# Block attention: weight halves prepared by GpSimd in the first stage; causal mask by a matmul, maxima and exponentials read from PSUM

## The chip, the cores and the metric

One core of a Trainium2 chip runs the whole program. The metric is the device time of one execution in microseconds (us), the median of the runs shown. Engines: PE (TensorE, matmuls), DVE (VectorE), ACT (ScalarE), POOL (GpSimd), SP (SyncE, which here issues every DMA, all on one queue, and computes nothing). In the profile's rows "bank" is one of eight PSUM banks of 128 x 512 fp32.

## The reference, cut to what matters

Two layers over 16 batches of 128 tokens with 256 features. Layer 0: a cross attention with 16 heads of size 8 over features as tokens (its scores are computed per batch element), then a mixture of 64 experts. Layer 1: an mLSTM, then a "block": layer norms, causal self attention with 16 heads of size 128 and rotary embedding, and a mixture of 4 experts. The change touches layer 1's block attention and, as a place for work, layer 0's attention. The block attention is

```python
q = (h @ wq + bq).reshape(b, s, H, HD).transpose(0, 2, 1, 3)      # H, HD = 16, 128; h: (16, 128, 256)
k = (h @ wk + bk).reshape(b, s, H, HD).transpose(0, 2, 1, 3)
v = (h @ wv + bv).reshape(b, s, H, HD).transpose(0, 2, 1, 3)
q = q * cos + _rotate_half(q) * sin
k = k * cos + _rotate_half(k) * sin
scores = jnp.einsum('bhqd,bhkd->bhqk', q, k) / math.sqrt(HD)
scores = jnp.where(causal[None, None], scores, jnp.finfo(jnp.float32).min)
probs = jax.nn.softmax(scores.astype(jnp.float32), axis=-1).astype(q.dtype)
out = jnp.einsum('bhqk,bhkd->bhqd', probs, v)
return out.transpose(0, 2, 1, 3).reshape(b, s, H * HD) @ wo + bo
```

## The kernel before, in words

Each engine has its own instruction list, written out by hand in a fixed order, and waits on semaphores (`wait_ge`). The stages follow each other: layer 0 attention (to about 350 us of the span), layer 0 experts (to about 945), mLSTM (to about 1091), block attention (to about 1689), block experts.

**Two halves.** The large products use fp32r matmuls with both operands split in two: hi, the value rounded to fp32r, and lo, the rest. `product` (line 63) makes three matmuls of it: hi x hi, hi x lo, lo x hi (lines 67, 68, 69). So a weight needs its hi and its lo half in SBUF before it is used.

**First stage, layer 0 attention** (`layer0_*`, lines 112 to 478). For each of the 16 batches PE computes scores twice. The first pass (`maxima`, line 204) gives each row's maximum on DVE; it runs 28 heads (`AHEAD`) ahead of the second pass (`exponentials`, line 232), whose scores ACT exponentiates. The maxima of a batch are turned by PE, copied by ACT, cut into three bf16 parts by POOL (lines 474 to 478, `max_split`), and put by three small DMAs (`max_rows`, line 153, source `a_mparts`) into rows 72 to 74 of the stacked queries `a_qs`, where the second pass adds them inside its matmul: PE waits for `max_in` before a batch's first exponentials. The stacked queries and keys of a batch come from scratch in HBM by six DMAs of 192 KB, three for queries (line 146) and three for keys (line 147), each into 24 partitions (`stack`); four batches are held (`A_RING`). SP's order in the main loop is: three maxima DMAs for batch b, then, once PE has done all exponentials of batch b-1 (`exp_scores`, line 144), the six DMAs of the stack for batch b+3, then the maxima of batch b+1, and so on. POOL does nothing else here once the stacks are prepared.

**Block attention** (`attention_*`, from line 1442). 64 steps, one for each chunk of four batches and each of the 16 heads. In step n PE does, in this order: queries and keys of n (12 matmuls of 512 columns), scores of n-1 (4 fp32 matmuls, two records each; line 1700), the values of one batch (6 of 512), the turning of the probabilities of n-3 (4), the weighing of the values for n-4 (8 records), and the projection of n-5 (12 of 256 columns). Beside them:

- SP loads the raw weights of a head (`b_raw_qk`, 256 KB; `b_raw_o`, 128 KB) three deep, and those of the values of four heads (`b_raw_v`, 512 KB) two deep.
- DVE rounds them to hi (`split_qk`, `split_o`, `split_v`; lines 1872, 1878, 1884), POOL subtracts for lo (`rest`, line 1978).
- ACT writes the half-swapped queries and keys (`b_turned`, line 1809), POOL multiplies them by the sine (line 1996), DVE makes bias plus cosine product (`b_straight`, line 1892) and adds the two (line 1938).
- DVE adds the mask to the scores of n-1 and writes them to SBUF (`b_probs`, line 1907; this frees the score bank), takes the maximum (line 1909) and scales it (line 1911); ACT takes exponentials of n-2 in place (line 1798) with their sums; POOL multiplies by the inverse sums (line 1999).
- DVE and ACT take turns in copying the turned probabilities; ACT rounds the weighed values (line 1837) and DVE makes their rest (line 1948).

Layer norms of later chunks ("input" pieces, from line 1646) and the gate of finished chunks ("gate" pieces) are spread over the steps, one piece a step. Square roots and exponentials need different tables on ACT.

Of the kernel before, what the change touches and what calls it, by code (L numbers as in the profile page):

```python
# [103 lines left out]

def layer0_semaphores(k):
    s = k.sems("a", "weights_in var root normed qk_sums v_sums qk_whole qk_rounded q_rest k_rest q_middle k_middle q_low k_low v_copied k_ones "
               "max_scores maxed max_turned max_copied max_split exp_scores exped cleared weighted sums_copied turned_back divided "
               "out_sums out_turned proj_sums projected added")
    return s, {n: [k.sem(f"a_{n}{i}") for i in range(count)] for n, count in (("q_out", A_SLOTS), ("k_out", A_SLOTS), ("stack_in", A_RING), ("max_in", A_RING))}


def layer0_sp(k, m, s, ring):
# [35 lines left out]

    def max_rows(b):
# [304 lines left out]
def layer0_pool(k, m, s, ring):  # L454
# [16 lines left out]
    for b in range(NB):  # L471
# [6 lines left out]
        pool.tensor_tensor(m.mparts[i][:, 2, :], m.mrow[i][:, :], m.mparts[i][:, 1, :], ALU.subtract).then_inc(s.max_split)  # L478

# [962 lines left out]
def attention_memory(k, stack):  # L1442
    sb = tensors(k, stack, "b")
    pair = lambda name, n: [sb(f"{name}_{half}", [P, n], F32R) for half in ("hi", "lo")]
    m = namedtuple("m", "raw_qk raw_o raw_v split_qk split_o split_v rope mask norm columns v turned straight probs peak peak_scaled total inv probsT outT")
    return m([sb(f"raw_qk{i}", [P, NQK]) for i in range(3)], [sb(f"raw_o{i}", [P, D]) for i in range(3)], [sb(f"raw_v{i}", [P, NV]) for i in range(2)],
             [pair(f"qk{i}", NQK) for i in range(2)], [pair(f"o{i}", D) for i in range(2)], [pair(f"vw{i}", NV) for i in range(2)],
             sb("rope", [P, 2, S]), sb("mask", [P, S]), norm_memory(sb, "first"), sb("first_columns", [P, DK, BANK]),
             [sb(f"v{i}", [P, CHUNK, GROUP * RD]) for i in range(2)], [sb(f"turned{i}", [P, 2, BANK]) for i in range(2)],
             [sb(f"straight{i}", [P, 2, BANK]) for i in range(2)], [sb(f"probs{i}", [P, CHUNK, S]) for i in range(3)],  # L1450
             *([sb(f"{n}{i}", [P, CHUNK]) for i in range(2)] for n in ("peak", "peak_scaled", "total", "inv")),
# [3 lines left out]
def block_semaphores(k):  # L1455
    s = k.sems("b", "small_in tables_in gate_in experts_in pad var root normed rows turned columns x_hi x_lo with_bo qk_hi qk_lo o_hi o_lo v_hi v_lo "
               "qk_sums qk_turned qk_straight qk_sine rotated score_sums masked peaked exps inverted normalised probs_turned probs_by_dve probs_by_act v_sums v_copied weighed "
# [836 lines left out]
```

## Time and profile before

| | us |
|---|---|
| median of 3 runs | 1828.59 |
| lowest, highest | 1820.28, 1829.84 |
| the profiled execution | 1817.43 |
| its span | 1816.1 |

The profile describes one execution, which is shorter than each of the runs in the table. Busy times of the engines lie beside each other. In its chain of waits each step goes back to what released the instruction; in rows of the timeline the square bracket is the idle time of the engine before the instruction and what ended it; "x" is how many instructions a row merges.

### The profile page before, as it was taken

Reading aid. Unit: us, or ns where it says so; the run is one execution under the profiler, and the core shown is the slowest. Engines: PE = TensorE matmul, PEld = TensorE weight load, DVE = VectorE, ACT = ScalarE, POOL = GpSimd, SP = SyncE. Lnnn points to the kernel's source line nnn. Section 1 sums busy time; section 2 is a strip of 40 time slices with the busy share of each in tenths; the row PEclk is TensorE's granted clock in tenths of the full one; section 3 lists DMA queues with packets and bytes.
Section 4 is the critical chain, followed back from the end, with each engine's and each line's share of the span. In section 5 each row is a group of like instructions: output and inputs, shape, how many; then the busy total and the mean of one; then the engine's idle time right before and its main releaser. Section 6 shows DMA issues by size and latency. Waiting matters only on the chain.

```text
span 1816.1 us, 30483 instructions
## 1 busy us (share of the span) xinstructions
PE 1606.5 (88%) x10932; PEld 1268.4 (70%) x10932; DVE 1259.6 (69%) x2321; ACT 1019.4 (56%) x2050; POOL 765.8 (42%) x575
## 2 busy tenths in 40 slices
PE   4379999789999999999986964899899999999898
PEld 2135555368888888888872533788787778888687
DVE  6458788378644455444445576999999999999454
ACT  4247777644433335333335653877776877677453
POOL 5200000024435333333330014798798688877000
PEclk9569899899999999999996987999999999999899
DMA  5613232243343333343400002123112111211220
GB/s 155 154 55 83 76 84 61 80 111 105 94 129 106 104 110 102 108 116 102 118 10 6 4 2 92 48 72 103 56 56 68 56 56 56 68 48 30 70 47 24
DMA packets 73349, 137.42 MB, mean 76 GB/s; under 512 B 12824, under 2 KB 41308, under 8 KB 70384
## 3 DMA queue, kind: packets, MB, share of 16 engines
q1 hardware_dynamic: 73200, 135.48, 26.4%
q8 instruction: 88, 1.44, 0.3%
q14 instruction: 61, 0.50, 0.1%
HBM read 125.70 MB, written 8.95 MB: 74 GB/s over the span
## 4 chain that ended last, share of the span: by engine, by line
PE 54%; DVE 19%; issue 9%; DMA 8%; ACT 6%; POOL 2%; SPq 1%; DVEq 0%; ACTq 0%; POOLq 0%
PE bank L67 13%; PE bank L69 13%; PE bank L68 13%; DMA a_qs<-a_mparts 5%; DVE b_straight L1938 3%; DVE b_straight L1892 2%; PE bank L246 2%; PE bank L232 2%; PE bank L204 2%; ACT b_turned L1809 2%; DVE b_peak L1909 2%; POOL e_hidden L944 1%; DVE b_probs L1907 1%; PE bank L1700 1%; PE bank L1732 1%
## 5 line engine op out<-in xcount | busy, mean ns | idle before, releaser
L944 POOL TENSOR_TENSOR e_hidden<-e_gated,e_comb_wide 128x512 f32<-128x512 f32 x132 | 211.0, 1599 | 346.7 <-DVE e_gated L909 331.1
L784 ACT CAST e_hidden_hi<-e_hidden 128x512 fp32r<-128x512 f32 x132 | 82.0, 622 | 320.6 <-POOL e_hidden L944 320.6
L902 DVE TENSOR_TENSOR e_hidden_lo<-e_hidden,e_hidden_hi 128x512 fp32r<-128x512 f32 x132 | 98.2, 744 | 209.8 <-ACT e_hidden_hi L784 209.8
L423 DVE TENSOR_REDUCE a_negmax<-bank 128x2 f32<-128x512 f32 x256 | 165.6, 684 | 64.6 <-PE bank L204 63.3
L69 PE MATMUL bank<-e_x_hi,e_weights_lo 128*128 128x512 f32 (+1 forms) x528 | 209.5, 397 | 0.0
L67 PE MATMUL bank<-e_x_hi,e_weights_hi 128*128 128x512 f32 (+1 forms) x528 | 208.4, 395 | 0.7 <-ACT e_comb_rows L744 0.7
L68 PE MATMUL bank<-e_x_lo,e_weights_hi 128*128 128x512 f32 (+1 forms) x528 | 208.4, 395 | 0.0
L1809 ACT ACTIVATE b_turned<-bank,b_swap_bias 64x512 f32<-64x512 f32 x256 | 174.9, 683 | 17.7 <-PE bank L69 12.9
L1996 POOL TENSOR_TENSOR b_turned<-b_turned,b_rope 128x512 f32<-128x512 f32 x128 | 167.5, 1329 | 5.3 <-ACT b_turned L1809 4.8
L340 ACT ACTIVATE a_exp<-bank 128x512 f32<-128x512 f32 x256 | 142.9, 596 | 42.8 <-PE bank L232 35.4
L69 PE MATMUL bank<-e_weights_hi,e_hidden_lo 128*128 128x256 f32 (+1 forms) x528 | 149.4, 283 | 0.0
L67 PE MATMUL bank<-e_weights_hi,e_hidden_hi 128*128 128x256 f32 (+1 forms) x528 | 148.2, 281 | 0.5 <-DVE e_hidden_lo L902 0.5
L68 PE MATMUL bank<-e_weights_lo,e_hidden_hi 128*128 128x256 f32 (+1 forms) x528 | 148.4, 281 | 0.0
L1938 DVE TENSOR_TENSOR b_straight<-b_straight,b_turned 128x512 f32<-128x512 f32 x128 | 140.5, 1136 | 0.0
L1798 ACT ACTIVATE b_probs<-b_probs,b_peak_scaled 128x128 f32<-128x128 f32 x256 | 99.7, 391 | 68.2 <-DVE b_peak_scaled L1911 68.1
L204 PE MATMUL bank<-a_ks,a_qs 72*128 72x256 bf16 x512 | 108.0, 297 | 31.0 <-DMA a_ks<-a_k_parts 13.2
L1978 POOL TENSOR_TENSOR b_qk_lo<-b_raw_qk,b_qk_hi 128x512 fp32r<-128x512 f32 x64 | 84.7, 1324 | 109.9 <-DVE b_qk_hi L1872 109.9
L909 DVE TENSOR_TENSOR e_gated<-e_silu,bank 128x512 f32<-128x512 f32 x132 | 90.5, 686 | 56.7 <-PE bank L69 44.2
L232 PE MATMUL bank<-a_qs,a_ks 75*128 75x256 bf16 x512 | 100.2, 280 | 21.0 <-DMA a_qs<-a_mparts 20.1
L69 PEld LDWEIGHTS bank<-e_x_hi,e_weights_lo 128*128 128x128 f32 (+1 forms) x528 | 98.7, 187 | 22.7
L67 PE MATMUL bank<-b_x_hi,b_qk_hi 128*128 128x512 f32 x256 | 103.0, 402 | 12.8 <-POOL b_qk_lo L1978 4.5
L67 PEld LDWEIGHTS bank<-e_x_hi,e_weights_hi 128*128 128x128 f32 (+1 forms) x528 | 99.4, 188 | 19.7 <-ACT e_comb_rows L744 1.1
(326 smaller groups left out, 4318.1 us busy)
## 6 DMA issues: line engine op xcount, KB each, us to landing
e_comb_wide<-e_combT SPq DMA_DIRECT2D x130, 256.0 KB, 4.0
e_raw<-in_e_weights SPq DMA_DIRECT2D x64, 384.0 KB, 4.5
b_raw_qk<-in_b_wqk SPq DMA_DIRECT2D x64, 256.0 KB, 2.8
a_qs<-a_q_parts SPq DMA_DIRECT2D x48, 192.0 KB
a_ks<-a_k_parts SPq DMA_DIRECT2D x48, 192.0 KB
b_raw_v<-in_b_wv SPq DMA_DIRECT2D x16, 512.0 KB, 3.8
b_raw_o<-in_b_wo SPq DMA_DIRECT2D x64, 128.0 KB, 2.0
moe_comb_wide<-b_comb_rows SPq DMA_DIRECT2D x16, 256.0 KB, 6.7
```

Of the source, the lines that this page charges most:

```text
L67: pe.matmul(out, w_hi, x_hi, start=start, stop=False, skip_group_check=True)
L68: pe.matmul(out, w_hi, x_lo, start=False, stop=False, skip_group_check=True)
L69: return pe.matmul(out, w_lo, x_hi, start=False, stop=stop, skip_group_check=True)
L204: last = pe.matmul(bank[:, qb * POS:(qb + 1) * POS], m.qs[r][0:TERM_ROWS, h, qb * P:(qb + 1) * P], m.ks[r][0:TERM_ROWS, h, :], start=True, ...
L232: last = pe.matmul(bank[:, kb * POS:(kb + 1) * POS], m.ks[r][0:ROWS, h, kb * P:(kb + 1) * P], m.qs[r][0:ROWS, h, :], start=True, stop=True)
L340: act.activation(m.expo[at % A_EXPS][:, :, :].rearrange("p k q -> p (k q)"), banks[2 + h % 2][:, :], ACT.Exp, scale=float(1 / np.sqrt(np.f ...
L423: dve.tensor_reduce(m.negmax[b % 2][:, h, :], banks[h % 2][:, :].rearrange("p (q n) -> p q n", q=2), AX.X, ALU.max, negate=True).then_inc( ...
L944: pool.tensor_tensor(m.hidden[i][0:rows, :], m.gated[i][0:rows, :], m.comb_wide[u % E_RING][0:rows, chunk * BANK:(chunk + 1) * BANK], ALU. ...
L1798: last = act.activation(w.probs[n % 3][:, b, :], w.probs[n % 3][:, b, :], ACT.Exp, scale=SCALE, bias=w.peak_scaled[i][:, b:b + 1], accum_o ...
L1809: last = act.activation(w.turned[i][dst:dst + half, which, :], banks[bank][src:src + half, :], ACT.Identity, bias=m.swap_bias[dst:dst + ha ...
L1938: dve.tensor_tensor(w.straight[n % 2][:, which, :], w.straight[n % 2][:, which, :], w.turned[n % 2][:, which, :], ALU.add).then_inc(s.rotated)
L1996: pool.tensor_tensor(x, x, w.rope[:, 1, :].unsqueeze(1).to_broadcast([P, CHUNK, S]), ALU.mult).then_inc(s.qk_sine)
```

## The change

**In the first stage**, 32 pieces of the block attention's weights (16 heads' qk, 8 half groups of v, 8 pairs of o; 256 KB each) are loaded into four slots of the otherwise unused `columns` tensor, split by POOL into a rounded copy and a rest, and both are stored to scratch in HBM (256 KB each). POOL does two pieces behind each batch's `max_split`; SP does the stores of the batch before and the loads of the batch after in `max_rows`.

```diff
+KEPT, KEPT_SLOTS, KEPT_EACH = 512, 4, 2
+def kept_of(b):
+    return range(KEPT_EACH * b, min(KEPT_EACH * (b + 1), 2 * RH))
 def layer0_sp(k, m, s, ring):
+    def load_kept(u):
+        r = u % KEPT_SLOTS
+        if u >= KEPT_SLOTS:
+            sp.wait_ge(ring["kept_out"][r], 2 * DMA * (u // KEPT_SLOTS))
+        sp.dma_start(kept_places(k, u, units[u][0].shape)[0], units[u][0]).then_inc(ring["kept_in"][r], DMA)
+    def store_kept(u):
+        low, high = kept_places(k, u, units[u][0].shape)
+        sp.wait_ge(s.kept_low, u + 1)
+        for dst, src in zip(units[u][1], (high, low)):
+            sp.dma_start(dst, src).then_inc(ring["kept_out"][u % KEPT_SLOTS], DMA)
+    def kept(b):
+        if b:
+            for u in kept_of(b - 1):
+                store_kept(u)
+            for u in kept_of(b + 1):
+                load_kept(u)
     def max_rows(b):
...
+        kept(b)
...
     for b in range(1, A_RING):
         stack(b)
+    for u in range(KEPT_SLOTS):
+        load_kept(u)
...
+    for u in kept_of(NB - 1):
+        store_kept(u)
+    for r in range(KEPT_SLOTS):
+        sp.wait_ge(ring["kept_out"][r], 2 * DMA * (2 * RH // KEPT_SLOTS))
 def layer0_pool(k, m, s, ring):
         pool.tensor_tensor(m.mparts[i][:, 2, :], m.mrow[i][:, :], m.mparts[i][:, 1, :], ALU.subtract).then_inc(s.max_split)
+        for u in kept_of(b):
+            whole, high = kept_places(k, u, (P, KEPT))
+            pool.wait_ge(ring["kept_in"][u % KEPT_SLOTS], DMA * (u // KEPT_SLOTS + 1))
+            pool.tensor_copy(high.bitcast(F32R), whole).then_inc(s.kept_high)
+            pool.wait_ge(s.kept_high, u + 1)
+            pool.tensor_tensor(whole.bitcast(F32R), whole, high, ALU.subtract).then_inc(s.kept_low)
```

**In the block attention**, SP fetches both halves straight into their two buffers, and the splitting on DVE and POOL goes. A fetch waits until PE has done with the buffer. The mask, as bf16, is added by a matmul of the identity that opens the score bank; the scale 1/sqrt(128) goes into the queries' rotary tables (`rope_q`); DVE's maximum and ACT's exponentials read the bank, which PE may overwrite only once the exponentials are done. ACT's wait for the small vectors moves from the stage's start to the input's piece 6.

```diff
 def attention_sp(k, m, w, s, ring, before):
+    def fetch(split, whole, n, fetched):
+        for i in range(2):
+            sp.dma_start(split[n % 2][i][:, :].bitcast(F32), whole[n % whole.shape[0], i]).then_inc(fetched[n % 2], DMA)
...
-        if n + 3 < B_STEPS:
-            load_qk(n + 3)
-        if 4 <= n <= B_STEPS:
-            load_o(n - 1)
-        if n % GROUP == 0 and n // GROUP + 2 < B_GROUPS:
-            load_v(n // GROUP + 2)
+        if 2 <= n + 1 < B_STEPS and n >= 1:
+            sp.wait_ge(s.qk_sums, 2 * n)
+            fetch(w.split_qk, k.qk_parts, n + 1, ring["qk_in"])
+        if 2 <= n - 4 < B_STEPS:
+            sp.wait_ge(s.proj_sums, n - 5)
+            fetch(w.split_o, k.o_parts, n - 4, ring["o_in"])
+        if n % GROUP == 0 and 2 <= n // GROUP + 1 < B_GROUPS:
+            sp.wait_ge(s.v_sums, n)
+            fetch(w.split_v, k.v_parts, n // GROUP + 1, ring["v_in"])
     def scores(n):
+        if n:
+            pe.wait_ge(s.exps, n)
+        else:
+            pe.wait_ge(s.constants, 2)
+        pe.matmul(banks[SC][:, :].rearrange("p (b s) -> p b s", b=CHUNK), w.ident_16[:, :], w.mask_16[:, :].unsqueeze(1).to_broadcast([P, CHUNK, S]),
+                  start=True, stop=False, skip_group_check=True)
         pe.wait_ge(s.rotated, 2 * (n + 1))
-        if n:
-            pe.wait_ge(s.masked, n)
...
     def exponentials(n):
...
-            last = act.activation(w.probs[n % 3][:, b, :], w.probs[n % 3][:, b, :], ACT.Exp, scale=SCALE, bias=w.peak_scaled[i][:, b:b + 1],
+            last = act.activation(w.probs[n % 3][:, b, :], banks[SC][:, b * S:(b + 1) * S], ACT.Exp, bias=w.peak[i][:, b:b + 1],
...
-    act.wait_ge(s.small_in, 4 * DMA)
     for piece in range(INPUT_PIECES):
+        if piece == 6:
+            act.wait_ge(s.small_in, 4 * DMA)
         input_chunk(0, piece)
...
-        dve.tensor_tensor(probs[:, :, :], by_batch(banks[SC][:, :]), w.mask[:, :].unsqueeze(1).to_broadcast([P, CHUNK, S]), ALU.add).then_inc(s.masked)
-        dve.wait_ge(s.masked, n + 1)
-        dve.tensor_reduce(w.peak[i][:, :], probs[:, :, :], AX.X, ALU.max, negate=True).then_inc(own.tick())
-        dve.wait_ge(own.sem, own.n)
-        dve.tensor_scalar(w.peak_scaled[i][:, :], w.peak[i][:, :], SCALE, None, ALU.mult).then_inc(s.peaked)
+    def peaks(n):
+        dve.wait_ge(s.score_sums, n + 1)
+        dve.tensor_reduce(w.peak[n % 2][:, :], by_batch(banks[SC][:, :]), AX.X, ALU.max, negate=True).then_inc(s.peaked)
```

## Rows read from the trace of the kernel before

**Rows 1.** The page: busy us, share of the span; the chain's shares by line.
```profile
PE 1606.5 (88%) x10932; PEld 1268.4 (70%) x10932; DVE 1259.6 (69%) x2321; ACT 1019.4 (56%) x2050; POOL 765.8 (42%) x575
PE bank L67 13%; PE bank L69 13%; PE bank L68 13%; DMA a_qs<-a_mparts 5%; DVE b_straight L1938 3%; DVE b_straight L1892 2%; PE bank L246 2%; PE bank L232 2%; PE bank L204 2%; ACT b_turned L1809 2%; DVE b_peak L1909 2%; POOL e_hidden L944 1%; DVE b_probs L1907 1%; PE bank L1700 1%; PE bank L1732 1%
```
**Rows 2.** Busy us in one stretch: PE, PEld, DVE, ACT, POOL, PE clock, DMA share, GB/s.
```profile
1270.00:1400.00 130.00, 118.98 (x741) 103.19 (x740) 127.27 (x227) 95.02 (x228) 107.79 (x79) 0.99 0.19 56
```
**Rows 3.** Timeline of SP's queue, first stage: start us, duration us, engine, line.
```profile
139.57 0.76 SPq L146 DMA_DIRECT2D a_qs<-a_q_parts  x1
146.82 1.83 SPq L153 DMA_DIRECT2D a_qs<-a_mparts  x3
154.34 0.75 SPq L146 DMA_DIRECT2D a_qs<-a_q_parts  x1
218.39 0.75 SPq L146 DMA_DIRECT2D a_qs<-a_q_parts  x1
```
**Rows 4.** Chain that ended last, first stage: start us, duration us, what.
```profile
148.06 8.04 DMA a_qs<-a_mparts
```
**Rows 5.** Timeline of PE, first exponentials of four batches.
```profile
140.91 0.39 PE L232 MATMUL bank<-a_qs,a_ks 75*128 75x256 bf16 x2 [0.97 <-DMA a_qs<-a_mparts]
156.15 0.39 PE L232 MATMUL bank<-a_qs,a_ks 75*128 75x256 bf16 x2 [1.43 <-DMA a_qs<-a_mparts]
200.70 0.61 PE L232 MATMUL bank<-a_qs,a_ks 75*128 75x256 bf16 x2 [2.13 <-DMA a_qs<-a_mparts]
306.05 0.39 PE L232 MATMUL bank<-a_qs,a_ks 75*128 75x256 bf16 x2 [0.89 <-DMA a_qs<-a_mparts]
```
**Rows 6.** Line 153 from 117 to 120 us, no stack in flight.
```profile
DMA to landing us min/median/max: 1.8/1.9/1.9
```
**Rows 7.** Busy us in stretches of the first stage, columns as in rows 2.
```profile
142.00:144.00 2.00, 2.00 (x27) 1.17 (x18) 1.17 (x3) 1.49 (x4) 0.00 (x0) 1.00 0.60 147
150.00:152.00 2.00, 2.00 (x19) 1.67 (x16) 1.74 (x5) 1.99 (x5) 0.00 (x0) 1.00 0.19 70
201.00:211.00 10.00, 10.00 (x65) 5.10 (x64) 4.29 (x8) 4.92 (x11) 1.11 (x3) 0.53 0.32 94
```
**Rows 8.** Timeline of PE, score matmuls of four block steps.
```profile
1121.91 1.16 PE L1700 MATMUL bank<-b_straight 128*128 128x128 f32 x8 [1.97 <-DVE b_straight L1938]
1239.40 1.05 PE L1700 MATMUL bank<-b_straight 128*128 128x128 f32 x8
1247.24 1.06 PE L1700 MATMUL bank<-b_straight 128*128 128x128 f32 x8
1672.80 1.16 PE L1700 MATMUL bank<-b_straight 128*128 128x128 f32 x8 [1.05 <-DVE b_straight L1938]
```
**Rows 9.** Groups by form, 1060 to 1620 us, DVE: busy us, mean ns | idle before.
```profile
L1872 DVE CAST b_qk_hi<-b_raw_qk 128x512 fp32r<-128x512 f32 x59 | 44.4, 753 | 0.0
L1911 DVE TENSOR_SCALAR b_peak_scaled<-b_peak 128x4 f32<-128x4 f32 x56 | 40.7, 726 | 1.9
L1907 DVE TENSOR_TENSOR b_probs<-bank,b_mask 128x512 f32<-128x512 f32 x56 | 36.8, 657 | 0.0
```
**Rows 10.** The page's groups, POOL.
```profile
L1978 POOL TENSOR_TENSOR b_qk_lo<-b_raw_qk,b_qk_hi 128x512 fp32r<-128x512 f32 x64 | 84.7, 1324 | 109.9 <-DVE b_qk_hi L1872 109.9
```
**Rows 11.** Chain that ended last, mLSTM stage, a bf16 matmul of 128x512.
```profile
1006.91 0.32 PE bank L1225
```
**Rows 12.** Timeline of ACT, one table load.
```profile
1284.58 1.28 ACT L1778 ACT_TABLE_LOAD   x1
```
**Rows 13.** Timeline of DVE at the start of the block attention.
```profile
1097.46 0.18 DVE L1657 RECIPROCAL b_first_rstd<-b_first_rstd 128x4 f32<-128x4 f32 x1 [4.06 <-ACT b_first_rstd L1778]
1117.87 3.99 DVE L1938 TENSOR_TENSOR b_straight<-b_straight,b_turned 128x512 f32<-128x512 f32 x2
```
**Rows 14.** The DMA view: the queue (packets, MB, share of 16 engines); an issue (us to landing).
```profile
q1 hardware_dynamic: 73200, 135.48, 26.4%
out<-resid SPq DMA_DIRECT2D x8, 256.0 KB, 2.2
```

More of the change, by code:

```diff
@@ L102, in layer0_memory, with kept_units, kept_places @@
         [sb(f"rstd{i}", [P, CHUNK]) for i in range(NCHUNK)])
+KEPT, KEPT_SLOTS, KEPT_EACH = 512, 4, 2
+def kept_units(k):
+    io, units = k.io, []
+    for h in range(RH):
+        units.append((io["b_wqk"][h], [k.qk_parts[h, i] for i in range(2)]))
+    for g in range(RH // GROUP):
+        for half in range(2):
+            cols = slice(half * KEPT, (half + 1) * KEPT)
+            units.append((io["b_wv"][g][:, cols], [k.v_parts[g, i][:, cols] for i in range(2)]))
+    for h in range(0, RH, 2):
+        units.append((io["b_wo"][h:h + 2].rearrange("h p n -> p h n"), [k.o_parts[h:h + 2, i].rearrange("h p n -> p h n") for i in range(2)]))
+    return units
+def kept_places(k, u, shape):
+    first = (u % KEPT_SLOTS) * 2 * KEPT
+    whole, high = (k.columns[:, :, :].rearrange("p k t -> p (k t)")[:, at:at + KEPT] for at in (first, first + KEPT))
+    return [t if len(shape) == 2 else t.rearrange("p (h n) -> p h n", h=shape[1]) for t in (whole, high)]
+def kept_of(b):
+    return range(KEPT_EACH * b, min(KEPT_EACH * (b + 1), 2 * RH))
 def layer0_semaphores(k):
@@ L1444, in attention_memory @@
     pair = lambda name, n: [sb(f"{name}_{half}", [P, n], F32R) for half in ("hi", "lo")]
[L1445 to L1448, printed above, removed]
+    m = namedtuple("m", "split_qk split_o split_v rope rope_q mask mask_16 ident_16 norm columns v turned straight probs peak total inv probsT outT")
@@ L1449, in attention_memory @@
+    return m([pair(f"qk{i}", NQK) for i in range(2)], [pair(f"o{i}", D) for i in range(2)], [pair(f"vw{i}", NV) for i in range(2)],
+             sb("rope", [P, 2, S]), sb("rope_q", [P, 2, S]), sb("mask", [P, S]), sb("mask_16", [P, S], BF16), sb("ident_16", [P, P], BF16), norm_memory(sb, "first"), sb("first_columns", [P, DK, BANK]),
              [sb(f"v{i}", [P, CHUNK, GROUP * RD]) for i in range(2)], [sb(f"turned{i}", [P, 2, BANK]) for i in range(2)],
              [sb(f"straight{i}", [P, 2, BANK]) for i in range(2)], [sb(f"probs{i}", [P, CHUNK, S]) for i in range(3)],
-             *([sb(f"{n}{i}", [P, CHUNK]) for i in range(2)] for n in ("peak", "peak_scaled", "total", "inv")),
+             *([sb(f"{n}{i}", [P, CHUNK]) for i in range(2)] for n in ("peak", "total", "inv")),
@@ L1683, in queries_keys @@
         pe.wait_ge(s.x_lo, chunk + 1)
-        pe.wait_ge(s.qk_lo, n + 1)
+        pe.wait_ge(ring["qk_in"][n % 2], 2 * DMA * (n // 2 + 1))
         for which, bank in ((0, Q), (1, K)):
@@ L1707, in values @@
         b = chunk * CHUNK + tile
-        pe.wait_ge(s.v_lo, group + 1)
+        pe.wait_ge(ring["v_in"][group % 2], 2 * DMA * (group // 2 + 1))
         if free:
@@ L1739, in project @@
         pe.wait_ge(s.out_lo, n + 1)
-        pe.wait_ge(s.o_lo, n + 1)
+        pe.wait_ge(ring["o_in"][n % 2], 2 * DMA * (n // 2 + 1))
         if h == 0 and chunk:
@@ L1987, in attention_pool @@
         input_chunk(0, piece)
-    pool.wait_ge(s.tables_in, 2 * DMA)
+    pool.wait_ge(s.constants, 2)
     for n in range(B_STEPS + 5):
-        if n + 1 < B_STEPS:
-            rest(w.raw_qk, w.split_qk, s.qk_hi, s.qk_lo, n + 1)
         if n < B_STEPS:
@@ L1995, in attention_pool @@
                 x = by_batch(w.turned[n % 2][:, which, :])
[L1996 removed]
+                pool.tensor_tensor(x, x, (w.rope if which else w.rope_q)[:, 1, :].unsqueeze(1).to_broadcast([P, CHUNK, S]), ALU.mult).then_inc(s.qk_sine)
         if 2 <= n <= B_STEPS + 1:
```

93 lines of the change are left out of this document (25 added, 68 removed).

## The prediction

> **What bounds the kernel now.** I read the page's busy shares first [rows 1]: PE is busy 88% of the span and no other engine is near it, but that mean covers five stages, and the change touches two. The page's chain of waits names one item that is no engine: 5% of the span, some 90 us, is the DMA that brings the maxima rows [rows 1]. Then the busy time by stretches [rows 2]: in the block stage DVE is busy 127.27 of 130 us (98%) where PE is busy 118.98, so DVE sets that pace.
>
> *The first stage's loop* is seen by laying three views side by side. SP issues the six DMAs of a stack at 139.57 and the three small maxima DMAs at 146.82 [rows 3]; the third of these lands only 8.04 us after its issue, at 156.10, and PE's next exponentials start at 156.15, after 1.43 us of idle [rows 4, 5]. The same small DMAs with no stack ahead of them land in 1.8 to 1.9 us [rows 6]. What holds them is the stack: the DMA share is 0.60 at 142 to 144 and 0.19 at 150 to 152 [rows 7], there some three of sixteen engines at work. So a stack's bytes lie unevenly, a few engines carry most of them, and the maxima wait behind these. PE is idle before the exponentials for that DMA in ten steady batches by 0.29 to 2.13 us [rows 5], so this loop has no slack: stack issued, about 15.8 us later the maxima land (139.57 to 156.15 is 16.6; ten such pairs run from 15.0 to 16.6, mean 15.8) [rows 3, 5], the batch of exponentials runs, the next stack goes out at 154.34, and so on. From the landing at 140.91 to that at 306.05 are 11 batches: 165.1 / 11 = 15.0 us each [rows 5].
>
> *The block stage.* PE's first score matmul comes 64 times, from 1121.91 to 1672.80: 550.9 / 63 = 8.74 us a step; its shortest steps are 7.84 us (1239.40 to 1247.24), and they recur whenever DVE is not late [rows 8]. So 7.84 us is PE's own work.
>
> **The change, block stage.** DVE loses per step the rounding of qk (753 ns), the mask addition (657) and the scaling of the peak (726) [rows 9], 2.1 us, and the rounding of o and a quarter of v beside: 98% of 8.74 is 8.6 us of DVE work, and at most 6.4 of it is left. The maximum now reads PSUM instead of SBUF; the addition that goes away read the same bank in 657 ns, so I cost it at 0, within 0.1 either way, and not on PE's path. POOL loses as many subtractions (1324 ns for qk) and keeps three operations of that size, 4.0 us [rows 10]. ACT keeps its instructions: 95.02 of 130 us [rows 2], 6.4 a step. The exponentials' source moves from SBUF to PSUM, cost 0: ACT has 1.7 us of room in 8.1, and 0.1 us either way on each of four fits in it. PE gains one 128x512 bf16 matmul per step. Such a matmul holds the chain for 0.32 us in the mLSTM stage [rows 11], the upper end; nearest below is one record of the eight score matmuls, 1.06 / 8 = 0.13 [rows 8]. I take 0.25, nearer to the one of its own shape. PE becomes the bound at 7.84 + 0.25 = 8.1 us.
>
> New waits there: the mask matmul waits until ACT has read the scores of the step before. ACT starts these after its out_hi, which follows the weighing; until the mask matmul PE still has the projection and the queries/keys, 24 of its 50 matmuls and so about 4 us, while ACT has five of its dozen instructions, about 2.5. That cover is gone only where a pair of table loads (2 x 1.28) [rows 12] stands between; nine such places at 1 us: up to 9, I take 5. The loads of both halves are issued once the step before last has left its buffer, 13 us ahead, for about 4 us of transfer. They double the stage's traffic from a share of 0.19 [rows 2] to about 0.4, which costs nothing.
>
> Sum: 63 steps x 8.1 = 510; the first four lack the weighing and the projection, a quarter of PE's work, about -6; side pieces on PE, some 30 small matmuls a chunk at 0.13 (1.06 / 8), three chunks, 12; table loads 5. That is 521 against 551: -30. At the stage's start ACT waits for the b_bo DMA, and DVE, its variance done, stands idle 4.06 us for ACT's root of 0.2 [rows 13]; the wait moves to a later piece: -3.8. The first two additions take 3.99 us beside POOL's subtractions [rows 13]; half of it should go: -2. The drain's five mask additions and scalings mostly ride beside PE: 0. Three small constants on DVE lie beside PE's first products. Together -36, between -44 (no table trouble, 7.96 us steps) and -20.
>
> **The change, first stage.** Added are 32 pieces: 32 loads and 64 stores of 256 KB on SP's one queue, and 64 POOL operations of 128x512. POOL first: its rows give 1.3 us for such an operation [rows 10], 5.3 a batch, in an engine that works 1.1 us a batch. It stands behind the maxima's split and is done long before the next one. Cost 0.
>
> SP's queue is the point. After the maxima DMAs of batch b it now (1) issues the four stores of batch b-1, (2) waits until each pair has landed, since the two loads for batch b+1 go into the same slots, (3) issues these, and only then (4) the next stack. The stores spread over all 16 engines, so a share of each lies behind the old stack and the maxima on the few slow ones: none is complete before the maxima landing M. A 256 KB store alone lands in 2.2 us against 1.9 for the 8 KB maxima: at least 0.3 us each; the page's 135.48 MB in 26.4% of 1816.1 us are 283 GB/s: 0.9 each [rows 6, 14]. I take 0.7, nearer to the page's mean over all transfers. Four stores: M + 2.8; the last load's issue 0.45, so the stack goes out at M + 3.3, where now it goes out 1.3 to 1.8 us before M. Then 15.8 us as now, and 0.3 for the load just ahead: the next M is 19.4 later, not 15.0. PE's batch (under 15, and 17.7 in the batch with the lowered clock: 200.70 to 218.39) [rows 3, 5] fits inside. So +4.4 us for each of 11 batches: +48. The first four loads stand between the first stacks and the first maxima: 4 x 0.7 = 2.8. Sum +51; with 0.3 a DMA (2.4 x 11 + 1.2) +28, with 0.9 (5.2 x 11 + 3.6) +61. Behind the last stack (three batches) nothing is held, and the closing wait for the stores ends before the experts' loads may start.
>
> The Trainium skill, "DMA: Bandwidth & Descriptors", section "Queues, rings and completion order", says that each DMA engine takes its descriptors in ring order and that a DMA's semaphore is complete only with all its engines; section "How many engines (k)" there, that a transfer is split over the largest number up to 16 that divides the slowest dimension of both sides, which for 3x8 rows would be 3 engines, for 128 rows 16. The 0.17 to 0.27 of rows 7 agrees; by that rule the stores are all held as I say, and without it (stores passing the stack) the first rival's sum holds.
>
> **Total.** 1817.4 us (span 1816.1) + 51 - 36 = 1832. The profiled execution was 11 us under the median of the runs shown, so 1844 beside 1828.6.
>
> **Rivals.**
> 1. *The stores are not held, and the block's gain stands alone.* SP now has 5.7 us between the third maxima DMA (148.65) and the next stack (154.34) [rows 3]. If the four stores land within about 3.5 us of the last issue, the stack is in time. That is the point of decision: a stack issue no later than PE's end of the batch. For it: a lone store lands in 2.2 [rows 14]. Against it: 6.9 to 8.7 us for maxima on the same queue at the same place. 1828.6 - 36 + 3 = 1796.
> 2. *The clock falls with the new idle.* After 2.13 us of idle at 200.70 the granted clock was 0.53 in 201 to 211 and that batch took 17.7 us instead of 13.4 [rows 3, 5, 7]. With over 4 us of idle in each batch it may stay low through one; twice 13.4 less what DVE and ACT hide is about 23, so 11 x (23 - 19.4) = 40 more: 1884.
> 3. *The block's PE does not reach its floor*: ACT in order, exponentials at its head, a late qk_turned in each step. 1828.6 + 51 = 1880, if nothing is gained. Against it: ACT was busy 95 of 130 us [rows 2].
> 4. *The weights' halves arrive late in the block* (two buffers, not three): about 1 us a step, 1828.6 + 51 - 36 + 60 = 1904; 13 us of lead speaks against it.
>
> **How the numbers follow.** Forecast 0.62, its own range 1813 to 1862 (the two sets of bounds); rival 1 0.20; rival 2 0.08; rival 3 0.08; rival 4 0.02. What a measurement of this kernel can tell is about 0.5%, 9 us: 1819 to 1838 is "same". The forecast's share is 0.03 faster, 0.10 same, 0.49 slower. So faster 0.23, same 0.10, slower 0.67. The range 1808 to 1881 takes in rival 3 and leaves out rival 1's centre and most of rival 2.
>
> **What will show it.** In SP's timeline the stack issue some 3 us after the maxima landing, and 19 to 20 us between batches' exponentials, PE idle 4 us or more before each; score matmuls in the block 8.0 to 8.2 us apart, DVE under 80% there; the block's first matmul about 4 us sooner after its start. Wrong: batches still at 15 us (rival 1), a clock of 0.5 through whole batches (rival 2), block steps above 8.5 (rivals 3 and 4).

## The result and the profile after

| | before | after |
|---|---|---|
| median of 18 runs each, us | 1822.62 (1805.01 to 1833.87) | 1830.82 (1826.04 to 1841.5) |
| ratio after / before, 95% interval | | 1.0062 [1.0039, 1.0086] |
| profiled execution: span, us | 1816.1 | 1828.1 |
| experts' first load issued (end of the first stage) | 350.45 | 391.76 (+41.3) |
| block's first load issued | 1091.38 | 1134.52 (+43.1) |
| first / last score matmul of the block | 1121.91 / 1672.80 | 1158.11 / 1682.27 (+36.2 / +9.5) |

The change made the kernel slower by 0.6%: 8 us between the medians, 12 between the profiled executions. The 12 are the sum of a loss of 41.3 us in the first stage, 1.8 in the stages between, 2.5 in the tail behind the block's last scores, and of gains of 6.9 us at the block's start and of 26.7 us over its 63 steps.

The page after: busy times, the clock in 40 slices, the queue and the chain, which answer to [rows 1, 14].
```profile
PE 1633.9 (89%) x10996; PEld 1279.5 (70%) x10996; DVE 1103.7 (60%) x2052; ACT 1007.5 (55%) x2050; POOL 609.9 (33%) x495
PEclk9568888889999999999998787899999999999799
q1 hardware_dynamic: 110832, 194.21, 35.9%
PE 69%; DMA 8%; DVE 7%; ACT 5%; issue 5%; SPq 3%; POOL 3%; POOLq 0%; ACTq 0%; DVEq 0%
```
The same two lines, the clock and the chain, before:
```profile
PEclk9569899899999999999996987999999999999899
PE 54%; DVE 19%; issue 9%; DMA 8%; ACT 6%; POOL 2%; SPq 1%; DVEq 0%; ACTq 0%; POOLq 0%
```
DVE and POOL lost 156 us of work each, and yet the end came later. DVE fell from 19% to 7% of the chain and PE took its place. The DMA had its 8% before, too; SP's queue rose from 1% to 3%.

The timeline of SP's queue in the first stage after, which answers to [rows 3] (start us, duration us, engine, line). L175 is the query stack, L184 the loads of the pieces, L190 their stores, L204 the maxima.
```profile
135.45 2.72 SPq L204 DMA_DIRECT2D a_qs<-a_mparts  x3
138.21 2.09 SPq L190 DMA_DIRECT2D b_qk_parts<-columns  x4
145.33 1.56 SPq L184 DMA_DIRECT2D columns<-in_b_wqk  x2
147.00 0.77 SPq L175 DMA_DIRECT2D a_qs<-a_q_parts  x1
151.93 2.85 SPq L204 DMA_DIRECT2D a_qs<-a_mparts  x3
154.82 2.23 SPq L190 DMA_DIRECT2D b_qk_parts<-columns  x4
164.17 2.29 SPq L184 DMA_DIRECT2D columns<-in_b_wqk  x2
166.57 0.77 SPq L175 DMA_DIRECT2D a_qs<-a_q_parts  x1
```
PE's first exponentials of four batches after, which answer to [rows 5]:
```profile
144.56 0.39 PE L290 MATMUL bank<-a_qs,a_ks 75*128 75x256 bf16 x2 [1.22 <-DMA a_qs<-a_mparts]
163.44 0.61 PE L290 MATMUL bank<-a_qs,a_ks 75*128 75x256 bf16 x2 [3.70 <-DMA a_qs<-a_mparts]
182.56 0.39 PE L290 MATMUL bank<-a_qs,a_ks 75*128 75x256 bf16 x2 [1.20 <-DMA a_qs<-a_mparts]
...
343.78 0.61 PE L290 MATMUL bank<-a_qs,a_ks 75*128 75x256 bf16 x2 [2.51 <-DMA a_qs<-a_mparts]
```
The maxima land at 144.56. The loads go out 0.8 us later, when the stores of 138.21 have landed, and the stack at 147.00; before, it went out 1.3 us ahead of the landing. From 144.56 to 343.78 are 11 batches of 18.1 us, where they were 15.0. Ahead of all of them but one PE waits for the maxima, by 0.22 to 4.38 us, so the loop of the queue still sets the pace.

The block after, by stretches (PE, PEld, DVE, ACT, POOL, clock, DMA share, GB/s; answers to [rows 2]), and, in PE's timeline, two of its steps (answers to [rows 8]).
```profile
1200.00:1300.00 100.00, 99.11 (x631) 85.95 (x630) 66.20 (x100) 74.47 (x188) 48.10 (x38) 1.00 0.46 148
```
```profile
1237.07 1.05 PE L1758 MATMUL bank<-b_straight 128*128 128x128 f32 x8
1245.16 1.05 PE L1758 MATMUL bank<-b_straight 128*128 128x128 f32 x8
```
DVE fell from 98% to 66%; PE, at 99%, is the bound, with 8.09 us from step to step (before, the shortest steps were 7.84 and the mean was 8.74).

### The profile page after: what moved, and what is told of

It reads as the page before. It is cut to its first block, busy times and chain, and to the rows that moved or that the text cites. A ratio compares the mean times of both kernels' runs of the same rounds, so it can differ in the third digit from the quotient of the medians.

```text
span 1828.1 us, 30253 instructions
## 1 busy us (share of the span) xinstructions
PE 1633.9 (89%) x10996; PEld 1279.5 (70%) x10996; DVE 1103.7 (60%) x2052; ACT 1007.5 (55%) x2050; POOL 609.9 (33%) x495
## 4 chain that ended last, share of the span: by engine, by line
PE 69%; DMA 8%; DVE 7%; ACT 5%; issue 5%; SPq 3%; POOL 3%; POOLq 0%; ACTq 0%; DVEq 0%
PE bank L67 16%; PE bank L69 16%; PE bank L68 16%; DMA a_qs<-a_mparts 6%; PE bank L1790 3%; PE bank L1758 3%; PE bank L304 2%; PE bank L290 2%; PE bank L262 2%; PE bank L1780 1%; POOL e_hidden L1008 1%; PE bank L1290 1%; PE bank L1289 1%; SPq L204 1%; PE bank L1300 1%
## 5 line engine op out<-in xcount | busy, mean ns | idle before, releaser
L1869 ACT ACTIVATE b_turned<-bank,b_swap_bias 64x512 f32<-64x512 f32 x256 | 174.9, 683 | 43.1 <-PE bank L69 39.3
L2018 POOL TENSOR_TENSOR b_turned<-b_turned,b_rope_q 128x512 f32<-128x512 f32 x64 | 82.8, 1294 | 258.8 <-ACT b_turned L1869 258.8
L290 PE MATMUL bank<-a_qs,a_ks 75*128 75x256 bf16 x512 | 108.0, 298 | 41.1 <-DMA a_qs<-a_mparts 40.2
L262 PE MATMUL bank<-a_ks,a_qs 72*128 72x256 bf16 x512 | 114.5, 312 | 33.0 <-DMA a_ks<-a_k_parts 13.7
L1935 DVE SCALAR_TENSOR_TENSOR b_straight<-bank,b_head_bias,b_rope_q 128x512 f32<-128x512 f32 x64 | 48.0, 749 | 111.2 <-ACT b_turned L1869 111.1
L68 PEld LDWEIGHTS bank<-e_x_lo,e_weights_hi 128*128 128x128 f32 (+1 forms) x528 | 98.7, 187 | 18.8
```

Source lines behind the costliest of these rows:

```text
L68: pe.matmul(out, w_hi, x_lo, start=False, stop=False, skip_group_check=True)
L262: last = pe.matmul(bank[:, qb * POS:(qb + 1) * POS], m.qs[r][0:TERM_ROWS, h, qb * P:(qb + 1) * P], m.ks[r][0:TERM_ROWS, h, :], start=True, ...
L290: last = pe.matmul(bank[:, kb * POS:(kb + 1) * POS], m.ks[r][0:ROWS, h, kb * P:(kb + 1) * P], m.qs[r][0:ROWS, h, :], start=True, stop=True)
L1869: last = act.activation(w.turned[i][dst:dst + half, which, :], banks[bank][src:src + half, :], ACT.Identity, bias=m.swap_bias[dst:dst + ha ...
```

## The experiments

**Each half of the change alone.** *first_stage_alone* is the kernel before with the 32 pieces (loads, POOL's operations, stores), which nothing reads; *block_alone* is the changed block with the first stage of before. Its scratch is filled in the experts stage by 64 stores of a finished tile, so the halves hold other values than the weights':
```diff
+                if u < 32:
+                    for i in range(2):
+                        sp.dma_start(fills(k, i)[u], m.x_split[1][:, 0, 0:512].bitcast(F32)).then_inc(ring["fill"][(2 * u + i) % 4], DMA)
```


> The kernel before with only the first stage's part of the change (32 pieces loaded, split by GpSimd and stored; nothing reads them later). Theory (SP waits for stores that are held behind the stack on a few DMA engines, so each next stack goes out late): batches 18.1 us apart instead of 15.0, the experts' first load 41 us later than in the kernel before, all later stages unchanged, total +41 us. Rival (the first stage is only part of it; the doubled traffic or the clock of later stages costs too): this kernel is less than 30 us slower than before.

> The changed block attention with the first stage as before; its halves' scratch is filled by 64 stores of a finished tile during the experts stage, so the values are not the weights' halves. Theory: steps of 8.09 us and the earlier start give 27 + 7 us, total -34 against before, the experts stage within 3 us. Rival (part of the block's 27 us comes from POOL and DMA work having been moved, or from the clock): outside -25 to -40.

Measured: 1860.87 us, ratio to before 1.0239 [1.0192, 1.0285], and 1787.46, ratio 0.9835 [0.9791, 0.9879]. Against the 1820.45 us of before beside them that is +40.4 and -33.0; they sum to +7.4, and the whole change measured +8.2: no action of the halves on each other is seen, to within the 8 to 9 us that each interval leaves. In the profiles the first stage alone has batches of 18.3 us and the experts' first load 41.7 us later than before; the block alone has its 63 steps in 522.8 us (550.9 before). Both are what the first theories said. How much one profiled execution differs from another shows in *block_alone*, too: its first stage is that of the kernel before, and it ended 4.7 us later (355.10 instead of 350.45).

**POOL's part of the first stage alone** (*pool_only*: the 64 operations, none of the DMAs; the slots are filled with ones by one GpSimd instruction at the program's start).

> The kernel before, with GpSimd's 64 additional operations of the first stage alone: the same two operations on the same two places of SBUF for each of the 32 pieces, but none of the loads and stores of the pieces, so the places hold no weights. Theory A (GpSimd has the room, and all of the first stage's loss came from the DMA queue): batches of 15.0 us as before and the kernel within 4 us of the kernel before. Theory B (GpSimd's new work slows VectorE, with which it shares SBUF, or delays its own work for the keys): batches of 15.5 us or more and 8 us or more above the kernel before.

Measured: 1825.18 us, ratio 1.0013 [0.9983, 1.0042]; the batches 15.1 us. The first stage is 2.2 us longer, all of it ahead of the first exponentials (113.20 instead of 110.93), where this kernel alone has that fill, 3.54 us. The loss is the queue's, not GpSimd's.

**Eight rows a DMA** (*before_spread*, *after_spread*: each query DMA of a stack cut in three).
```diff
-            sp.dma_start(flat(m.qs[r], 3 * t, 3), parts_of("q")[t].unsqueeze(0).broadcast_to([3, HD, HEADS * POS])).then_inc(ring["stack_in"][r], DMA)
+            for j in range(3):
+                sp.dma_start(flat(m.qs[r], 3 * t + j, 1), parts_of("q")[t]).then_inc(ring["stack_in"][r], DMA)
```


> The kernel before with each query DMA of a stack (24 rows, source repeated three times) issued as three DMAs of 8 rows; the same bytes. Theory (a few engines carry most of the stack and the maxima DMAs wait behind it): the stack's bytes lie on more engines, the maxima land before PE ends the batch, no idle before the first exponentials, batches 13.4 to 13.8 us apart instead of 15.0, the first exponentials some 5 to 8 us earlier, total -20 to -25 us. Rival (PE bounds this stage and the maxima's wait costs nothing more than the 1 us seen): at most -5 us, or slower by SP's twelve issues instead of six.

> The changed kernel with the stack's query DMAs split in the same way. Theory: the stores are no longer held, SP's wait ends before PE ends the batch, batches 13.6 to 14.5 us apart instead of 18.1, total -45 to -55 against the changed kernel, so about -40 against before. Rival (SP's wait for the stores alone is the cost, whatever lies on the engines): batches stay above 16.5 us, gain under 20 us.

Measured: 1811.55 us, ratio 0.9979 [0.9949, 1.0009], batches of 14.2 us; and 1812.15, ratio to before 0.9961 [0.9928, 0.9994], batches of 17.2, some 18 us under the changed kernel. The first isn't clear of the noise (9 us between the medians, 12 between the profiled spans), and of the second it is the rival's numbers that came (batches above 16.5 us, under 20 us gained). The theory, by which the cut frees the queue, failed in both. The stretches from the stack's issue on show why, for before and before_spread (columns as above):
```profile
143.00:145.00 2.00, 2.00 (x18) 1.37 (x15) 1.88 (x5) 1.69 (x4) 0.00 (x0) 1.00 0.71 135
149.00:151.00 2.00, 2.00 (x24) 1.50 (x15) 1.29 (x3) 1.58 (x5) 0.00 (x0) 1.00 0.25 85
151.00:153.00 2.00, 2.00 (x26) 1.08 (x24) 1.80 (x6) 1.90 (x4) 0.00 (x0) 1.00 0.17 70
```
```profile
138.00:140.00 2.00, 2.00 (x18) 1.47 (x17) 1.70 (x5) 1.69 (x4) 0.00 (x0) 1.00 0.68 82
140.00:142.00 2.00, 2.00 (x27) 1.07 (x25) 1.44 (x3) 1.60 (x6) 1.12 (x3) 1.00 0.86 107
146.00:148.00 2.00, 2.00 (x26) 1.24 (x26) 1.80 (x5) 1.99 (x5) 0.00 (x0) 1.00 0.51 74
```
Before ends in a tail of three busy engines (0.17 of 16), each 8 KB packet in 0.31 us. The eight-row DMAs keep 8 to 14 engines busy and move no more: most of their packets take 0.6 to 1.4 us. (Only in the stack's first 2 us, 136 to 138, did they move 147 GB/s, at a share of 0.83.) From its first to its last 8 KB packet a stack takes 12.9 us before and 12.3 in before_spread, the mean of twelve each. So the idle engines were not all of it, and the cut cost nearly what it brought.

**Another order of the stack's rows** (*before_by_dim*, *after_by_dim*): same six DMAs of 24 rows on the same places, but a source with 8 outermost. `q` with `broadcast_to([3, HD, ...])` reads the eight rows three times over; `broadcast_to([HD, 3, ...])` reads each row three times in a row. The keys change their order with the queries, since the two must match.
```diff
-            sp.dma_start(flat(m.qs[r], 3 * t, 3), parts_of("q")[t].unsqueeze(0).broadcast_to([3, HD, HEADS * POS])).then_inc(ring["stack_in"][r], DMA)
-            sp.dma_start(flat(m.ks[r], 3 * t, 3), parts_of("k")).then_inc(ring["stack_in"][r], DMA)
+            sp.dma_start(flat(m.qs[r], 3 * t, 3), parts_of("q")[t].unsqueeze(1).broadcast_to([HD, 3, HEADS * POS])).then_inc(ring["stack_in"][r], DMA)
+            sp.dma_start(flat(m.ks[r], 3 * t, 3), parts_of("k").rearrange("t d f -> d t f")).then_inc(ring["stack_in"][r], DMA)
```


> The kernel before, with the rows of the stacks in another order: within each group of 24 rows the eight dimensions of a head are the outer index and the three repeats the inner one, for queries and keys alike. Number, size and destination of the DMAs (six of 24 rows of 8 KB) stay, the sum over rows is the same; only the outermost dimension of the source is 8 where it was 3. In the kernel before, a stack's packets go at 17 to 20 a microsecond at first and end in a tail in which three DMA engines alone are busy, 12.9 us in all. Theory A (the query DMAs, whose source has 3 as its outermost dimension, run on three engines, and these set the stack's time): the tail goes, the stack needs about 8 us, the maxima behind it are not late any more, PE's batches are at their work of 13.5 to 14.5 us where they were 15.0, and the kernel gains 8 to 20 us. Theory B (the few SBUF rows that a 24-row DMA reaches set the time, or the query's rows being read three times): the destinations are the same, so nothing changes beyond 3 us.

Measured: 1779.65 us, ratio 0.9773 [0.9735, 0.9811]: 41 us less in the medians and 33 between the profiled spans (1816.1 and 1782.8), where at most 20 was expected. The stack's stretches, and SP's queue:
```profile
123.00:125.00 2.00, 2.00 (x17) 1.47 (x18) 1.62 (x5) 1.64 (x4) 0.00 (x0) 1.00 0.55 193
125.00:127.00 2.00, 2.00 (x26) 1.05 (x25) 1.44 (x4) 1.60 (x6) 1.07 (x3) 1.00 0.52 152
127.00:129.00 2.00, 2.00 (x22) 1.20 (x23) 1.97 (x6) 1.91 (x4) 0.05 (x1) 1.00 0.55 150
129.00:131.00 2.00, 2.00 (x28) 1.38 (x17) 1.29 (x4) 1.58 (x4) 0.00 (x0) 1.00 0.31 82
131.00:133.00 2.00, 2.00 (x24) 1.31 (x26) 1.81 (x6) 1.99 (x5) 0.00 (x0) 1.00 0.03 6
```
```profile
127.08 1.82 SPq L153 DMA_DIRECT2D a_qs<-a_mparts  x3
134.59 0.71 SPq L146 DMA_DIRECT2D a_qs<-a_q_parts  x1
140.86 1.19 SPq L153 DMA_DIRECT2D a_qs<-a_mparts  x2
```
Some eight engines (0.52 to 0.55 of 16) carry it at 150 to 193 GB/s, and the long tail of three is gone: a stack takes 8.4 us from its first to its last 8 KB packet, the mean of twelve, and not 12.9. Maxima go out every 13.8 us (the last row shows two of three), and from 100 us on PE never waits for them, where it waited 20.1 us before, 10.0 of these ahead of the first batch. It is busy 100.00 us of 100 at clock 1.00 between 100 and 200, and every batch from 107 to 286 takes 13.8 us: that is PE's own work, and the queue sets the pace no longer. The first stage is 34 us shorter. The batches give 13.5 of these, within the 8 to 20 expected. 19 lie ahead of the first exponentials (91.88 instead of 110.93), behind the first four stacks; that is what the expectation had left out. The Trainium skill, "DMA: Bandwidth & Descriptors", section "Why a DMA increments its semaphore by 16 and not by 1", under "How many engines (k)", says that a DMA goes over the largest number of engines up to 16 that divides the slowest dimension of both its sides. By that rule it would be, as an estimate, 8 for this source and 3 for the old one of the queries, and the shares of 0.55 and 0.17 agree. As queries and keys changed together, what each gave isn't known.

> The changed kernel with the stacks' rows in the order that gained 40 us on the kernel before (query DMAs with 8 as the outermost dimension of their source, where it was 3). Theory A (in the changed kernel too the stack's landing, 12.9 us, and the maxima behind it are in every batch's circle, and the shorter stack leaves room for the pieces): batches of 13.5 to 15 us where they were 18.1, and 40 to 60 us less than the changed kernel, so 1770 to 1790. Theory B (the pieces' own traffic is what holds the batches): batches of 16 us and more, and less than 30 us gained.

Measured: 1761.46 us, ratio to before 0.969 [0.9644, 0.9736], some 68 us under the changed kernel, where 40 to 60 were expected; batches of 14.35, within theory A's 13.5 to 15. Between the two kernels with the new order the first stage differs by 12.0 us (experts' first load at 316.43 and 328.48) where it differed by 41.3: with the new order the change is a gain (0.969 against 0.9773 without the change, 15 us, and 15 between the profiled spans; the two intervals just touch). Of the 12.0 us, 6.0 lie ahead of the first exponentials, and most of the rest in one batch of 17.91 at a granted clock of 0.72; nearly all others take 13.8 to 14.2. Most of what the pieces cost was the tail. That the gain is 15 and not the block's 34 less 12 comes from the untouched stages between, which took 6 us more in this profiled execution (746.0 and 739.8).

**The loads a batch later** (*late_loads*: the changed kernel; the loads stand ahead of the stores, behind the next maxima).
```diff
+        if b >= 2:
+            for u in kept_of(b):
+                load_kept(u)
         if b:
             for u in kept_of(b - 1):
                 store_kept(u)
-            for u in kept_of(b + 1):
-                load_kept(u)
```


> The changed kernel, with the loads of a batch's two kept pieces issued one batch later, ahead of that batch's stores: SP then never waits for stores that it has only just issued. Amounts and sizes of all DMAs stay. In the changed kernel the stack went out 2.4 to 3.1 us after the maxima had landed and a batch took 18.1 us. Theory A (a batch is the time until the stack goes out, plus the stack's landing, plus the maxima behind it): the stack goes out within 1 us of the release of its ring place, a batch takes 16 to 17 us, and the kernel is 12 to 22 us faster than the changed kernel. Theory B (what the pieces move through the same queue lengthens the stack and the maxima, whenever it is issued): the batches stay within 0.4 us of 18.1, and the kernel within 5 us of the changed one.

Measured: 1808.65 us, ratio to before 0.9928 [0.9889, 0.9967], 22 us under the changed kernel, at theory A's upper end; batches of 16.3 us, PE's wait for the maxima 27.8 us between 100 and 350 instead of 40.2. So 1.8 of the 3.1 us that a batch had grown were SP's wait for its own stores. What the remaining 1.3 are isn't shown. In two of the 11 batches, of 18.6 and 18.9 us, the granted clock was 0.73 (before, in one of 17.9, it was 0.72), and the one behind the first of them took 18.0. The other eight take 15.5 in the mean, where before without its slow one took 14.7, so the pieces' traffic in the queue explains 0.8 us of a batch at most.

**The mask on VectorE again** (*dve_mask*: the changed kernel without the mask matmul; VectorE adds the mask and writes the scores to SBUF, and its maximum and ACT's exponentials read them there).
```diff
-        pe.matmul(banks[SC][:, :].rearrange("p (b s) -> p b s", b=CHUNK), w.ident_16[:, :], w.mask_16[:, :].unsqueeze(1).to_broadcast([P, CHUNK, S]),
-                  start=True, stop=False, skip_group_check=True)
+        dve.tensor_tensor(probs[:, :, :], by_batch(banks[SC][:, :]), w.mask[:, :].unsqueeze(1).to_broadcast([P, CHUNK, S]), ALU.add).then_inc(s.masked)
```


> The changed kernel, with the causal mask added by VectorE into SBUF as in the kernel before, maxima and exponentials read from there, and no mask matmul on TensorE; the weights' halves still come ready-made. In the changed kernel most score steps take 8.09 us, which is PE's own work with the mask matmul of 0.39 us in it, and PE waits 9.1 us in all for the exponentials ahead of that matmul. Theory A (PE is the bound and VectorE at 92 per cent just fits): steps of 7.85 us at most places, and 5 to 15 us less than the changed kernel. Theory B (VectorE, with 0.8 us more of work in each step, is the bound or hands its results to PE late): steps of 8.1 us and more, no gain or up to 15 us more than the changed kernel.

Measured: 1809.86 us, ratio to before 0.9938 [0.9907, 0.997], 21 us under the changed kernel (16 between the profiled spans, 1828.1 and 1812.0), above the 5 to 15 expected. Steps of 7.83 us in PE's timeline:
```profile
1238.20 1.06 PE L1754 MATMUL bank<-b_straight 128*128 128x128 f32 x8
1246.03 1.06 PE L1754 MATMUL bank<-b_straight 128*128 128x128 f32 x8
```
63 steps take 505.8 us instead of 524.2. VectorE, the bound before, has room for the addition (busy 70.80 us of the 100 from 1200 on); put on PE, the bound after, it costs 18 us. In these 18 are two things that no run separates: the matmul's own place in the step, 0.26 us (8.09 less 7.83), and PE's wait ahead of it until the exponentials have been read from the bank, 9.1 us in all. With the mask on VectorE that wait is gone, and 2.6 us of waiting for `b_straight` come in its place.

**The edits together** (*by_dim_late_loads*, and with the mask on VectorE).

> The changed kernel with the stacks' rows in the new order and the pieces' loads one batch later, mask on TensorE as changed. If the two edits of the first stage act on one circle, the second has little left to gain: 0 to 8 us less than with the new order alone, batches of 13.4 to 14 us. If SP's wait for its own stores still holds the stack back by 2 to 3 us a batch, the loads' place gains 15 us or more. Expected 1760 to 1785, 35 to 60 us under the kernel before.

> The kernel of the run before it in this call, with the mask added by VectorE into SBUF and no mask matmul. On the changed kernel this edit gained 15 to 20 us. If that gain belongs to the block alone, it is found again whole here: 1745 to 1770. If it was in part a clock or an overlap that came with the slow first stage, it is less than 8 us.

Measured: 1765.06 us, ratio 0.9714 [0.9665, 0.9763], batches of 13.8: the loads' place brings nothing that can be measured on top of the row order. With the mask on VectorE 1751.09, ratio 0.9627 [0.958, 0.9674], 14 us less, and 63 steps in 504.6 us where they were 522.3: the block's gain of 18 us is found again in the steps, and this kernel is 68 us under the one before and some 79 under the changed one.

**Rows nine apart** (*before_strided*: what slowed the eight-row DMAs? 18 DMAs of eight rows stand in place of the six).
```diff
+            for j in range(3):
+                rows = slice(3 * t + j, TERM_ROWS, 9)
+                sp.dma_start(m.qs[r][rows, :, :].rearrange("p h n -> p (h n)"), parts_of("q")[t]).then_inc(ring["stack_in"][r], DMA)
+                sp.dma_start(m.ks[r][rows, :, :].rearrange("p h n -> p (h n)"), parts_of("k")[j]).then_inc(ring["stack_in"][r], DMA)
```


> The kernel before, its stacks loaded by 18 DMAs of eight rows of 8 KB (nine for the queries as in before_spread, nine for the keys, where that kernel has three of 24 rows), and the eight rows of each lie nine SBUF rows apart instead of side by side. In before_spread the DMA engines were busier than in the kernel before (share 0.68 to 0.86 in the first 4 us) and moved less (82 to 107 GB/s), and the batches were 14.1 us. Theory A (eight neighbouring rows are what makes a packet slow): with rows spread over 72 partitions 150 GB/s and more, the stack in 8 to 9 us, batches of 13.8 us and PE without idle time ahead of the exponentials, 15 us and more under before_spread, so 1780 to 1795. Theory B (the number of DMAs, or reading the same few rows of DRAM from several engines, makes it slow): 80 to 110 GB/s again, batches of 14.1 us and more, within 8 us of before_spread or above it (18 issues on SP take 6 us of each batch).

Measured: 1815.38 us, ratio 0.9983 [0.9951, 1.0015], batches of 14.35. Theory B's numbers came (its 80 to 110 GB/s, batches of 14.1 us and more, within 8 us of before_spread), and of its causes the number of DMAs, by another way than slow packets: the packets are quick again (0.31 to 0.55 us), yet through most of the stack only 78 to 119 GB/s move, with a share of 0.26 to 0.41, because each issue holds SP for 0.60 us, 18 of them 11.6 us and not the 6 that I had counted:
```profile
141.76 0.60 SPq L148 DMA_DIRECT2D a_qs<-a_q_parts  x1
142.40 0.60 SPq L149 DMA_DIRECT2D a_ks<-a_k_parts  x1
```
With some 5 engines at work instead of 8 to 14 the quick packets may come from the rows' distance or from the smaller crowd. What slows eight neighbouring rows stays open. The Trainium skill, "SBUF — State Buffer", "Door 1: The DMA port swizzle (why `[64,N]` ≈ `[32,N]`)", has a formula from the partition to one of 16 ports, by which eight neighbouring rows that start at a multiple of eight lie on two; the runs fit it and don't prove it.

## Why the prediction was right

The forecast was 1844 us beside 1828.6, slower by 0.8%; measured were 1830.82 beside 1822.62, slower by 0.45% (0.6% by the ratio). In the profiled executions the forecast was +15 us (+51 - 36), and +12.0 came. Path and cause were right in both stages. That the sum came so near is in part luck: the first stage was forecast 10 us too dear, the block's gain 2 us too large, and 4 us came that the sum didn't have. The effect is the small difference of two large ones and barely above the 0.5% that the prediction called "same".

- *First loads, +2.8:* +3.4 (first exponentials at 110.93 and 114.33).
- *A batch of 19.4 us, +48 over 11:* 18.1 us, +34.1. This is the term that was too large, by both of its parts: the stack at M + 3.3 was at M + 2.4 to 3.1 in the four batches from 144.56 on, mean 2.6, so a store cost nearer to 0.5 than to 0.7; and the 16.1 from there to the next maxima were 18.1 - 2.6 = 15.5. Its direction and cause stand by *late_loads* (SP's wait) and by the new order: in *after_by_dim* the loads go out 5.0 to 6.6 us after the stores' first issue (five batches from 106.19 on; 134.67 and 141.28 are one such pair), in the changed kernel 7.1 to 9.7 us (five from 138.21 on). Its lower bound is summed wrong: 0.3 a DMA instead of 0.7 takes 1.6 from the 4.4 and leaves 2.8, not 2.4, so +32 and not +28. Nor do the bounds give the forecast's own range: 1828.6 + 61 - 20 is 1870, not 1862. Neither changes the forecast.
- *Behind the last stack nothing is held, 0:* +3.6 (M of batch 13 to the experts' first load 44.4 and 48.0 us), so here the prediction left a term out, and it is the clock. Behind the idle time of 2.51 us at 343.78 PE was busy without a gap to 361.68, 17.9 us at a mean granted clock of 0.72; before, that batch took 13.6 at 1.00 (306.05 to 319.68). With it the first stage is 3.4 + 34.1 + 3.6 = 41.1, of the 51 forecast, within its bounds of 28 to 61.
- *POOL 0:* right by *pool_only*, batches of 15.1 beside 15.0.
- *Three engines carry most of a stack, by the share of 0.17 to 0.27:* right for the tail, and worth more than I saw. (Rows 7 show 0.19 of it; in the stack's second half, from 147 to 153, the share was 0.17 to 0.25, three to four engines.) I used it for the place of the stores only and did not ask what the tail cost the kernel before: 41 us.
- *PE's floor in the block 7.84 + 0.25 = 8.1:* 8.09. The mask matmul's own record is longer, 389 ns: records of neighbouring matmuls overlap (those of 128x512 beside a step last 0.39 us and start every 0.23). The last figures of each row are the idle time before it and what ended it:
```profile
L1754 PE MATMUL bank<-b_mask,b_ident 128*128 128x512 bf16 x62 | 24.1, 389 | 9.3 <-ACT b_probs L1858 9.1
L1858 ACT ACTIVATE b_probs<-bank,b_peak 128x128 f32<-128x128 f32 x248 | 87.4, 371 | 2.2 <-DVE b_peak L1947 2.0
```
- *Table loads in front of the mask matmul, 5 of at most 9:* 9.1 us, the upper end, at eight places (2.31 at one and 0.88 to 1.19 at seven). *Steps 521 us:* 524.2, so -26.7 and not -30.
- *Start of the block -3.8 and -2:* -6.9. The wait for ACT's root fell from 4.06 to 0.33 us, the first two additions from 3.99 to 1.82:
```profile
1136.89 0.18 DVE L1711 RECIPROCAL b_first_rstd<-b_first_rstd 128x4 f32<-128x4 f32 x1 [0.33 <-ACT b_first_rstd L1836]
1155.99 1.82 DVE L1968 TENSOR_TENSOR b_straight<-b_straight,b_turned 128x512 f32<-128x512 f32 x2
```
- *Exponentials from PSUM, 0:* right for the time. An exponential went from 391 to 371 ns and its accumulator read from 188 to 212.
- *Not in the sum:* +1.8 us in the stages between and +2.5 in the tail.

The rivals. *Not held* (1796): the stores were complete only after the maxima had landed (loads issued at 145.33); refuted by SP's timeline. *The clock stays low* (1884): half of it came. The granted clock of 100 to 300 us fell from 0.91 and 0.95 to 0.81 and 0.83, and the batches were still 18.1 us: PE's batch at that clock still fits behind the DMAs, if only just (ahead of one batch PE waited 0.22 us, ahead of another not at all). Where nothing of the queue stood in its way, behind 343.78, the clock cost the 4.3 us above. *PE not at its floor* and *halves late*: refuted by 8.09 us steps.
```profile
100.00:200.00 100.00, 78.08 (x686) 44.94 (x685) 60.91 (x125) 57.31 (x117) 27.48 (x39) 0.81 0.42 132
200.00:300.00 100.00, 88.63 (x773) 50.16 (x774) 64.41 (x134) 63.35 (x132) 26.70 (x41) 0.83 0.51 154
```
And before:
```profile
100.00:200.00 100.00, 84.93 (x827) 50.50 (x826) 72.02 (x150) 68.01 (x141) 6.69 (x18) 0.91 0.26 70
200.00:300.00 100.00, 95.66 (x939) 56.57 (x940) 77.70 (x163) 75.73 (x159) 7.81 (x21) 0.95 0.31 82
```

## What to carry to other kernels

Work moved off the busiest engine of one stage is paid for in the stage that takes it: look there for the circle that has no slack, here a queue and not an engine, and price each new DMA by the waits that SP does between the old ones. A DMA share of 0.17 while someone waits for the queue is a finding of its own: look at the outermost dimension of the source before moving anything else. And when an engine is relieved, don't put the work on the one that becomes the bound: VectorE fell from 98% to 66% while PE at 99% took the mask, with the wait ahead of it, for 18 us.

## What the runs showed of the hardware

- The same bytes to the same tile, with 8 instead of 3 as the outermost dimension of the source: by the share some 8 engines instead of a tail of 3, a stack in 8.4 us instead of 12.9 from its first to its last packet.
- More engines busy was not more moved: eight-row DMAs at a share of 0.86 and 107 GB/s, 24-row DMAs at 0.55 and 150 GB/s. Why is open.
- The issue of an eight-row DMA held SP for about 0.3 us with neighbouring rows (0.94 to 1.10 for three) and for 0.60 with rows nine apart.
- A batch of the first stage that takes PE 13.8 us at a granted clock of 1.00 took 17.9 at a mean of 0.72, with PE busy all the time or nearly so (before, 200.70 to 218.61; after, 343.78 to 361.68; after_by_dim, 211.57 to 229.49), behind 2.13, 2.51 and 1.59 us in which PE was idle.
